# First attention of a two-layer transformer block: x read with its last two axes exchanged, instead of turned on the PE

## What is computed

```
x   = LN(x + MHA16(x, ctx; d=64, score bias side[b], key mask))         # stages L0a and L0b, 8 heads each
x   = LN(x + MHA16(x, x;   d=32, pair mask))                            # stage SA
x   = LN(x + MHA16(x, ctx; d=32))                                       # stage CA
out = LN(x + W2 relu(W1 x))                                             # feed-forward
```

## Time and profile before

| what | us |
|---|---|
| runs, median of 3 | 4939.62 (4936.41 to 4939.77) |
| span of the profiled execution | 4938.0 |
| PE busy | 4462.8 (90%) |
| DVE busy | 3497.3 (71%) |
| ACT busy | 2779.7 (56%) |
| POOL busy | 2480.3 (50%) |
| mean granted clock of the PE | 0.960 |
| turning matmuls of all stages into psJ (512 of L579) | 94.4 |

### The profile page before, as it was taken

How to read it: one execution, slowest core, us unless ns; L and a number is a source line. 1 busy time by engine, 2 the same in 40 slices (tenths; PEclk the granted TensorE clock), 3 DMA queues, 4 the chain that set the end, 5 groups by cost and what they waited for, 6 DMA issues and landing times. The chain is left out here.

```text
span 4938.0 us, 81172 instructions
## 1 busy us (share of the span) xinstructions
PE 4462.8 (90%) x22656; PEld 3435.4 (70%) x22656; DVE 3497.3 (71%) x8408; ACT 2779.7 (56%) x5985; POOL 2480.3 (50%) x3046
## 2 busy tenths in 40 slices
PE   7999999799999968989998987888899886999998
PEld 5777777577777746667776765666667664788887
DVE  5666666577777768888888886888888887233333
ACT  5555565455555547777777765777777776111111
POOL 3444444344444437777777764777777774000010
PEclk9999999899999979999999998999999998999999
DMA  2211111211111120000000001001110002010010
GB/s 82 71 45 45 49 59 52 77 50 66 45 45 45 39 86 14 27 26 13 26 20 22 24 35 58 24 29 35 35 35 21 32 24 95 26 47 30 26 46 30
DMA packets 110844, 203.76 MB, mean 41 GB/s; under 512 B 12416, under 2 KB 12416, under 8 KB 110592
## 3 DMA queue, kind: packets, MB, share of 16 engines
q1 hardware_dynamic: 110592, 201.13, 12.2%
HBM read 159.14 MB, written 41.94 MB: 41 GB/s over the span
## 5 line engine op out<-in xcount | busy, mean ns | idle before, releaser
L1213 POOL TENSOR_SCALAR PR<-PR,RS 128x512 f32<-128x512 f32 x1536 | 1078.4, 704 | 1107.1 <-DVE RS L1021 925.1
L814 ACT ACTIVATE R<-psT 128x512 fp32r<-128x512 f32 x1536 | 915.9, 596 | 1201.1 <-PE psT L622 1179.6
L1195 POOL TENSOR_SCALAR QS<-QK 32x1024 fp32r<-32x1024 f32 (+2 forms) x1152 | 1168.3, 1014 | 571.9 <-DVE QK L970 226.8
L808 ACT ACTIVATE PR<-PR,MN 128x512 f32<-128x512 f32 x1536 | 1102.3, 718 | 116.6 <-DVE MN L955 63.3
L955 DVE CUSTOM_DVE_ANT_0 PR<-psS,RAW 128x512 f32<-128x512 f32 x1024 | 702.5, 686 | 528.0 <-PE psS L606 401.6
L1013 DVE TENSOR_TENSOR R<-psT,R 128x512 fp32r<-128x512 f32 x1536 | 1029.8, 671 | 5.4 <-ACT R L814 5.4
L622 PE MATMUL psT<-ID,PR 128*128 128x128 f32 x6144 | 958.0, 279 | 79.5 <-POOL PR L1213 76.0
L636 PE MATMUL psV<-R 128*64 128x512 f32 (+1 forms) x3072 | 914.7, 422 | 82.9 <-DVE OG L982 82.6
L622 PEld LDWEIGHTS psT<-ID,PR 128*128 128x128 f32 x6144 | 746.2, 143 | 282.9 <-POOL PR L1213 138.1
L636 PEld LDWEIGHTS psV<-R 128*64 128x64 f32 (+1 forms) x3072 | 460.9, 160 | 341.1 <-issue 90.5
L609 PE MATMUL psS<-QS 96*128 96x512 f32 x1024 | 508.8, 497 | 96.5 <-POOL QS L1195 96.3
(11 more groups left out here) (101 smaller groups left out, 8551.4 us busy)
## 6 DMA issues: line engine op xcount, KB each, us to landing
RAW<-in_w SPq DMA_DIRECT2D x96, 256.0 KB, 4.4
RAW<-in_ctx_t SPq DMA_DIRECT2D x96, 256.0 KB, 2.9
x<-Y SPq DMA_DIRECT2D x96, 256.0 KB, 2.0
RAW<-x SPq DMA_DIRECT2D x96, 256.0 KB, 2.7
Y<-x SPq DMA_DIRECT2D x96, 256.0 KB, 3.8
RAW<-in_x SPq DMA_DIRECT2D x64, 256.0 KB, 3.1
RAW<-in_side SPq DMA_DIRECT2D x64, 256.0 KB, 2.7
Y<-in_x SPq DMA_DIRECT2D x32, 256.0 KB, 4.2
```

Source lines behind the costliest of these rows:

```text
L808: nc.scalar.activation(PR[:, k % 4], PR[:, k % 4], ACT.Exp, bias=MN[:, k % 8:k % 8 + 1], scale=-1.0, accum_out=SM[:, k % 8:k % 8 + 1]).the ...
L814: nc.scalar.activation(PT[h % 2][:, 0, :, qt * P:(qt + 1) * P], turned(st, k).rearrange("p (k t) -> p k t", k=NT), ACT.Copy).then_inc(t_hi, 1)
L1195: nc.gpsimd.tensor_scalar(to, pair, 1.0, 1.0, ALU.mult, ALU.mult).then_inc(stacked, 1)
L1213: nc.gpsimd.tensor_scalar(PR[:, k % 4], PR[:, k % 4], RS[:, k % 8:k % 8 + 1], 1.0, ALU.mult, ALU.mult).then_inc(p_ready, 1)
```

## The change

`Stage.turned_x` holds for the stages whose source is x, L0a and L0b. For them the host passes `x_t`, x with its two last axes exchanged, as a further input. SP loads 128 columns of x for all 512 tokens into a RAW slot (`load_turned_x`), ACT copies the slot to xT's hi part and DVE subtracts, both straight from RAW. X_TURN is left out, and so is its use of the psJ ring. As DVE is now the last reader of a RAW slot, the load of the tile two later waits for the new semaphore xs_lo, and JOB Q0 waits for it too. Slots, order of steps, and the stages SA, CA and the feed-forward stay as they are; the residual still comes from x.

```diff
--- before
+++ after
@@ -24,6 +24,7 @@
         self.src, self.res, self.dst = src, res, dst
         self.context, self.bias, self.norm, self.eps = context, bias, norm, eps
         self.rows, self.cols = rows, cols
+        self.turned_x = src == "x"
         self.heads = AD // dk
         self.per_group = P // dk
         self.steps = self.heads * NT
...
@@ -133,7 +134,8 @@
         job(("V", 1, 1), [32, 33, 34, 35])
     for tt in range(NT):
         x_at = -12 + tt if wide else -18 + tt + 2 * (tt // 2)
-        add(x_at, "X_TURN", tt)
+        if not st.turned_x:
+            add(x_at, "X_TURN", tt)
         add(x_at, "X_HI", tt)
         add(x_at + 1, "X_LO", tt)
         add(x_at - 6 if tt < 2 else x_at - (1 if wide else 3), "LOAD_X", tt)
...
@@ -365,8 +368,9 @@
         def counts(st):
 
             T, H = st.steps, st.heads
-            return dict(xs=NT, x_hi=NT, cs=KT, cs_hi=KT, cs_lo=KT, s=T, s_full=T, exp=T, recip=T, p=T, t=T, t_hi=T,
-                        pv=H, pv_half=H, pv_evac=H, o_hi=NG, o_lo=NG, j=2 * NG + 3 * NT, j_own=2 * NG + 3 * NT,
+            jobs = 2 * NG + (2 if st.turned_x else 3) * NT
+            return dict(xs_lo=NT, xs=NT, x_hi=NT, cs=KT, cs_hi=KT, cs_lo=KT, s=T, s_full=T, exp=T, recip=T, p=T, t=T, t_hi=T,
+                        pv=H, pv_half=H, pv_evac=H, o_hi=NG, o_lo=NG, j=jobs, j_own=jobs,
                         j_hi=2 * NG + NT, stack=H, pieces=3 * H, mask=1, mask_ready=1, side=NT, side_ready=NT, res=NT, y=NT, mv=NT,
                         var=NT, rstd=NT, y_norm=NT, gain=NT, y_done=NT, y_sum=NT)
 
...
@@ -426,6 +430,13 @@
                 sp.dma_start(xs[:, tal["xs"].slot(i)], dram[src][b, tt * P:(tt + 1) * P, :]).then_inc(
                     tal["xs"].sem_of(i), 16)
 
+            def load_turned_x(b, kt):
+                tal["x_hi"].next()
+                n = tal["xs_lo"].next()
+                sp.wait_ge(xs_lo, tal["xs_lo"].done(n - 2))
+                i = tal["xs"].next()
+                sp.dma_start(xs[:, tal["xs"].slot(i)], x_t[b, kt * P:(kt + 1) * P, :]).then_inc(tal["xs"].sem_of(i), 16)
+
             def load_w(src):
                 n = tal["w_lo"].next()
                 sp.wait_ge(w_lo, tal["w_lo"].done(n - 8))
...
@@ -456,6 +467,8 @@
             def ahead(st):
 
                 sp.wait_ge(x_hi, tal["x_hi"].done(tal["x_hi"].n - 1))
+                if st.turned_x:
+                    sp.wait_ge(xs_lo, tal["xs_lo"].done(tal["xs_lo"].n - 1))
                 if st.context:
                     sp.wait_ge(cs_lo, tal["cs_lo"].done(tal["cs_lo"].n - 1))
                 sp.wait_ge(s_evac, tal["s"].done(tal["s"].n - 1))
...
@@ -643,7 +660,9 @@
                     if part == 0:
                         n = tal["j"].next()
                         tal["j"].mark(name)
-                        if name == ("Q", 0):
+                        if name == ("Q", 0) and st.turned_x:
+                            pe.wait_ge(xs_lo, tal["xs_lo"].done(tal["xs_lo"].marked(NT - 1)))
+                        elif name == ("Q", 0):
                             pe.wait_ge(j_evac, tal["j"].done(tal["j"].marked(("x", NT - 1))))
                         if name == ("K", 0) and st.context:
                             pe.wait_ge(cs_lo, tal["cs_lo"].done(tal["cs_lo"].marked(NT - 1)))
...
@@ -682,6 +701,10 @@
                             values(*k)
                         elif step == "JOB":
                             job(*k)
+                        elif step == "X_LO" and st.turned_x:
+                            tal["xs"].next()
+                            tal["xs_lo"].next()
+                            tal["xs_lo"].mark(k)
                         elif step == "C_LO":
                             tal["cs_lo"].next()
                             tal["cs_lo"].mark(k)
...
@@ -813,6 +836,8 @@
                             act.wait_ge(t_full, tal["t"].done(n))
                             nc.scalar.activation(PT[h % 2][:, 0, :, qt * P:(qt + 1) * P],
                                                  turned(st, k).rearrange("p (k t) -> p k t", k=NT), ACT.Copy).then_inc(t_hi, 1)
+                        elif step == "X_HI" and st.turned_x:
+                            split_hi(xT[:, 0, k], xs, "xs", x_hi)
                         elif step == "X_HI":
                             x_hi_part(k, psJ, "j", j_full)
                         elif step == "C_HI":
...
@@ -883,6 +909,7 @@
             dve.sem_inc(acc_evac, NT)
             dve.sem_inc(w_lo, 8)
             dve.sem_inc(cs_lo, 2)
+            dve.sem_inc(xs_lo, 2)
             dve.sem_inc(h_lo, 4)
 
             def gate():
...
@@ -1012,6 +1039,8 @@
                             hi, lo = (PT[h % 2][:, p, :, qt * P:(qt + 1) * P] for p in range(2))
                             nc.vector.tensor_tensor(lo, turned(st, k).rearrange("p (k t) -> p k t", k=NT), f32(hi),
                                                     ALU.subtract).then_inc(t_evac, 1)
+                        elif step == "X_LO" and st.turned_x:
+                            split_lo(xT[:, 1, k], xT[:, 0, k], xs, 2, "x_hi", x_hi, xs_lo)
                         elif step == "X_LO":
                             tal["j_own"].next()
                             x_lo_part(k, psJ, "j", j_evac)
...
@@ -1199,7 +1228,7 @@
                         if step == "SCORE":
                             tal["s"].next()
                             tal["s"].mark(k)
-                        elif step in ("J_LO", "X_LO", "OUT_SUM"):
+                        elif step in ("J_LO", "OUT_SUM") or step == "X_LO" and not st.turned_x:
                             tal["j"].next()
                             tal["j"].mark(k)
                         elif step == "STACK":
...
@@ -1257,6 +1286,7 @@
     columns = lambda v: v.reshape(-1, P).T
     arrays = {
         "x": a["x"],
+        "x_t": a["x"].transpose(0, 2, 1),
         "ctx_t": a["ctx_1024"].transpose(0, 2, 1),
         "side": a["fside_Bx1xSxS2_0"],
         "key_mask": a["mask_Bx1x1xS2_ik0"].reshape(B, 1, 1, S),
```

More of the change, by code:

```diff
@@ L241, in turns, with build @@
         t.marks = {k: v + per * (count - 1) for k, v in t.marks.items()}
-def build(nc, x, ctx_t, side, key_mask, pair_mask, w, rows, cols, out):
+def build(nc, x, x_t, ctx_t, side, key_mask, pair_mask, w, rows, cols, out):
     import concourse.bass as bass
@@ L316, in build @@
         x_hi = sem("x_hi")
+        xs_lo = sem("xs_lo")
         w_hi = sem("w_hi")
@@ L396, in stage_loop @@
             per = counts(st)
-            names = names + (["cs", "cs_hi", "cs_lo"] if st.context else [])
+            names = names + (["cs", "cs_hi", "cs_lo"] if st.context else []) + (["xs_lo"] if st.turned_x else [])
             names = names + (["mask", "mask_ready", "side", "side_ready"] if st.bias == "side" else [])
@@ L413, in _ @@
         def _(sp):
-            tal = dict(xs=RingTally(xs_full), x_hi=Tally(x_hi, credit=2), cs=RingTally(cs_full),
-                       cs_lo=Tally(cs_lo, credit=2), ws=RingTally(ws_full), w_lo=Tally(w_lo, credit=8),
+            tal = dict(xs=RingTally(xs_full), x_hi=Tally(x_hi, credit=2), xs_lo=Tally(xs_lo, credit=2),
+                       cs=RingTally(cs_full), cs_lo=Tally(cs_lo, credit=2), ws=RingTally(ws_full), w_lo=Tally(w_lo, credit=8),
                        s=Tally(s_evac, credit=2), side=RingTally(side_full), side_ready=Tally(side_ready),
@@ L498, in run @@
                         elif step == "LOAD_X":
-                            load_x(st.src, b, k)
+                            if st.turned_x:
+                                load_turned_x(b, k)
+                            else:
+                                load_x(st.src, b, k)
                         elif step == "LOAD_C":
@@ L554, in _ @@
         def _(pe):
-            tal = dict(xs=RingTally(xs_full), w_lo=Tally(w_lo, credit=8), cs_lo=Tally(cs_lo, credit=2), s=Tally(s_evac, credit=2),
+            tal = dict(xs=RingTally(xs_full), xs_lo=Tally(xs_lo, credit=2), w_lo=Tally(w_lo, credit=8),
+                       cs_lo=Tally(cs_lo, credit=2), s=Tally(s_evac, credit=2),
                        p=Tally(p_ready), t=Tally(t_evac, credit=2), pv=Tally(pv_evac, credit=1),
@@ L741, in _ @@
         def _(act):
-            tal = dict(ws=RingTally(ws_full), cs=RingTally(cs_full), t=Tally(t_full), s=Tally(s_evac, credit=2), pv=Tally(pv_full),
+            tal = dict(ws=RingTally(ws_full), xs=RingTally(xs_full), cs=RingTally(cs_full), t=Tally(t_full), s=Tally(s_evac, credit=2), pv=Tally(pv_full),
                        o_lo=Tally(o_lo, credit=1), pv_evac=Tally(pv_evac, credit=1), j=Tally(j_full),
@@ L833, in run @@
                             tal["stack"].mark(k[0])
-                stage_loop(act, tal, st, ["t", "s", "pv", "o_lo", "pv_evac", "j", "stack"], run)
+                stage_loop(act, tal, st, (["xs"] if st.turned_x else []) +
+                           ["t", "s", "pv", "o_lo", "pv_evac", "j", "stack"], run)
             tal.update(u=Tally(u_full), h=Tally(h_lo, credit=4))
```

## The result

The changed kernel took 4963.8 us (median of four runs, 4957.9 to 4968.9) beside 4939.7 for the kernel before: ratio 1.0048, 95% interval 1.0034 to 1.0063. Run again beside the last experiment it took 4957.2 us, ratio 1.0037 (1.0024 to 1.0051). So it is slower by 16 to 24 us, 0.4 to 0.5%. The forecast was 4943, with a range that ended at 4963; the first measurement lies just above it. The profiled execution has a span of 4956.1 us, the shortest of those four, 18.1 above the span before.

A forecast was written before the change was run, and what follows sets the result against it. PE paces a batch as a whole, but DVE paces slots 20 to 24. Terms +10.8 (L0a and L0b's first batch change), -5 (L0b's other six) and -2.5 (prologues) give +3.3 us: 4943 us, range 4921 to 4963.

The forecast's parts named there:

- What bounds slots 20 to 24: Around the turns of the next batch, DVE sets the pace and its X_LO(3) releases Q0, for which PE waits 0.95 us.
- Turns: Four turning groups leave PE, 1.6 us a batch change; Q0 in L0a starts about 0.25 us earlier, not 2.8.
- The conflict with POOL: X splits now reading SBUF may meet POOL's work; 0.15 us on DVE's path, bounds 0 and 0.9.
- The clock: In L0a, emptier PE makes the granted clock fall at Q0; 1.6 us a batch change, bounds 0 and 2.5.
- L0b, -5: Six batch changes of L0b: Q0 1.6 us sooner, less 0.8 for clock falls; -5 us together, bounds -10 and +5.
- Prologues, -2.5: Starts of L0a and L0b, without turns on each tile's path: -1.9 and -0.6, together -2.5 us, bounds -4 and -1.
- the slower one: Rival: the clock falls for the long stretch at every Q0 in L0a and L0b; +21, 4960 us, chance 0.20.

The follow-up runs named there:

- the last experiment: Changed kernel with x's loads, copies and splits one slot earlier plus seven spare matmuls a batch in L0a and L0b, run again; 4918.9 us, ratio 0.9957.
- g_short_turns: Kernel before, with each turn in L0a and L0b doing one of its four transposes; 4935.7 us, ratio 0.9991.
- e_fill: Changed kernel plus spare PE work before Q0 in L0a and L0b, eight transposes and five 512-column matmuls a batch; 4933.1 us, ratio 0.9987.
- second profile: Profile of the changed kernel's second run, with no further change; its span is 4955.0 us.
- e_l0b: Changed kernel with only L0b reading the exchanged x, L0a turning it on PE as before; 4944.1 us, ratio 1.0009.
- e_l0a: Changed kernel with only L0a reading the exchanged x, L0b turning it on PE as before; 4952.9 us, ratio 1.0028.

## Why the prediction was wrong

**What bounds slots 20 to 24: right.** DVE was busy for 4.77 of 4.80 us and PE waited for the three things named, in that order. g_short_turns shows that in L0a PE's time there is worth about a third of itself, while the clock holds. In L0b it was worth more.

**Turns, "not 2.8 us" but 0.25 sooner: right in kind, 0.35 us off.** With the clock held (e_fill) the period is 0.1 longer than before instead of 0.25 shorter. The next term is what it missed.

**The conflict with POOL, 0.15 us: too small.** It was the term chosen near a single row. X_LO(1) lost 0.19 and X_LO(3) 0.44 in the batch shown, 0.6 together, and POOL's multiply and pieces lost as well; taking it away was worth 0.8 us a period, part of it through the clock. The Trainium skill ("SBUF — State Buffer", section "SBUF: two separate sides") has the pair of ports held for a whole instruction by whoever starts first. The trace agrees nearly: X_LO(3) had 0.57 us of POOL's piece in front of it, and of the 0.57 + 0.67 = 1.24 us of a full wait and a split behind it 1.11 was seen. In the kernel after, each of the 67 splits with two SBUF inputs that began with more than 0.2 us of a POOL multiply or piece left took what was left plus 0.53 to 0.55 us. The prediction had weighed this rule of the Trainium skill, by which the whole 0.25 us went, and then discounted it; the rule was nearer to what came.

**The clock: right that it falls at Q0; the step "I take 1.6, the short stretch, as dense work follows at once" failed.** The fall cost 2.0 us a batch, because in most batches the low stretch was some 6.8 us long and not 3.4: in five of the seven of L0a, that of the window of 531.6 above among them, though dense work stood behind it. The price of a short one was right: the periods behind the two short stretches were 106.2 and 106.4, 1.4 and 1.6 over e_fill's. The net per batch change of L0a was 12.9 / 7 = 1.8 (2.1 in the second profile) instead of 1.35.

**L0b, -5: wrong, and the largest miss.** The step that failed is "in about half of the batches I expect it to fall at Q0 too". Q0 did come sooner: with the clock held there (e_fill) the period fell from 109.2 to 107.9, 1.3 of the 1.6 forecast, and some 0.5 of that is a shorter low stretch in front of Q0, since the two batches of e_fill with a stretch as long as before took 108.4 and 108.5. But after the change the clock fell at Q0 in six of seven batches, and in five of these in both places of the same batch, behind PE's wait of 1.85 us for the head sum and again behind the one of 2.19 for Q0. Two windows of the kernel after, and the batch behind the one Q0 over which the clock held:

```profile
1203.90:1207.20 3.30, 3.30 (x10) 2.37 (x10) 3.30 (x9) 2.18 (x5) 2.10 (x3) 0.50 0.04 15
1214.20:1217.50 3.30, 3.30 (x11) 2.54 (x9) 2.48 (x6) 0.74 (x4) 2.11 (x4) 0.50 0.00 0
...
1542.30:1650.30 108.00, 102.72 (x497) 76.15 (x497) 78.91 (x186) 60.10 (x130) 49.15 (x65) 0.98 0.16 51
```

That batch took 108.0 us where those behind a Q0 with both falls took 109.4 to 109.6, so the fall over Q0 costs about 1.5 us. Before, the one low stretch of 6.7 us lay where DVE set the pace; now half of it lies over Q0. Seven batch changes gave +1.8 (+3.7 in the second profile) where -3.7 was forecast (+1.35 and -5).

**Prologues, -2.5: about right.** L0a's first Q0 came 2.5 us sooner against 1.9 forecast; as it came at 29.8 us in e_l0b, whose L0a is that of before, up to 0.8 of that may be scatter. In L0b, from the end of the last weights' split to Q0, 12.8 us became 12.2, and 11.3 in the second profile, against 0.6 forecast. What grew beside it in the +0.4 of the table lies before that, in the end of L0a and the weights. In the first profile ACT waited for tile 3's load, issued at 910.33:

```profile
910.33 0.33 SPq L438 DMA_DIRECT2D RAW<-in_x_t  x1
...
914.77 0.63 ACT L776 ACTIVATE xT<-RAW 128x512 fp32r<-128x512 f32 x1 [2.58 <-DMA RAW<-in_x_t]
```

4.4 us passed from issue to use, not the 2.85 of the earlier trace rows. In the second profile, with the same loads right behind it, it was 3.3, so the 4.4 is no fixed price of this place.

**What was left out.** In the first profile the end of L0b and SA's prologue took 3.1 us more, and the unchanged rest 2.4. This is scatter for the most part: in the second profile of the same kernel the two are +1.2 and -0.4, and in e_l0a, whose L0b is that of before, the rest took 3124.7 us as well. These stretches run with the clock low for part of the time, and how the low stretches happen to lie differs from execution to execution. The first median also lies 5.9 us above the time of its profiled execution (4957.9), the second 0.4 above its own (4956.8). The 4963.8 that fell just outside the range is the upper of the two medians; by its profiles the change costs 17 to 18 us where +3.3 was forecast, and L0a and L0b together account for 8.9 of the 14.8 us missed in the first profile and for 12.6 of 13.7 in the second.

Of the rivals it was the slower one, at 4960 us, that came nearest, and its mechanism is the one seen: a low stretch lies over Q0 in every batch of L0a, the long form in five of seven. It had 0.20. That its number came so near is in part luck, since it had the long form in L0b too, where it asked for 7.7 us and 1.8 to 3.7 were seen.

## What to carry to other kernels

Before taking work off the busiest engine, look whether that engine is the bound in the very stretch where the work stands, and then what it will do with the time: here PE's turns became waiting, and 2 us a batch were lost by the clock behind it. Give freed PE time to work that is moved forward, or fill it with matmuls that nobody reads, and measure both; the change was clearly worth keeping only once its splits stood a slot earlier, which the exchanged layout made possible. A source that moved from PSUM to SBUF cost nothing alone (0.67 and 0.68 us), but where GpSimd was busy for 3.87 of 4.80 us it made two engines wait for each other. And take a second profile of the same kernel before explaining a difference of 2 or 3 us in a stretch whose code did not change.

## What was not expected of the hardware

Thirteen spare matmuls and transposes a batch, some 1.9 us of PE time, made the changed kernel 24 to 31 us faster. A DVE split with two SBUF inputs took 0.68 us alone, 0.86 when POOL's instruction had 0.32 us to run and 1.11 when it had 0.57, and the same 0.68 when it had 0.14. Beyond 0.2 us left, the length was what was left plus 0.53 to 0.55 in all 67 cases of the kernel after: the last seventh of a microsecond of a conflict did not show.
